# Opening of an adaptive-norm transformer block: the late conditions as one four-group product, and the queue order of the second unit's weights

## The reference

```
ada = cond @ ada_w + ada_b                       # cond 32x256, ada_w 256x1536
shift1, scale1, gate1, shift2, scale2, gate2 = split(ada, 6)
x1  = ln(x) * (1 + scale1) + shift1              # x 32x32x256
qkv = x1 @ qkv_w + qkv_b                         # 16 heads of 128
x   = x + gate1 * (softmax(q k' / sqrt(128)) v @ out_w + out_b)
x2  = ln(x) * (1 + scale2) + shift2
x   = x + gate2 * (gelu(x2 @ ffn_w1 + ffn_b1) @ ffn_w2 + ffn_b2)
out = x0 + w3q(silu(w1q(x)) * w2q(x))            # x0 the input; ternary weights, 8-bit activations
```

## Time and profile before

| | |
|---|---|
| median of 3 runs | 326.51 us (326.22 to 327.21) |
| the profiled execution | 326.65 us, of which the span from first to last instruction is 324.5 us |
| TensorE busy | 314.2 us, 97% of the span |
| VectorE, ScalarE, GpSimd busy | 224.2, 183.6 and 125.4 us |
| granted TensorE clock | 1.000 over the span |
| data moved by DMA | 24.41 MB, mean 75 GB/s |

### The profile page before, as it was taken

One profiled execution on the slowest core, in us unless ns is written; L12 is line 12 of the kernel. 1 busy time (PEld: TensorE's weight loads), 2 busy tenths in 40 slices (PEclk: granted clock), 3 DMA queues, 4 the chain that ended last, 5 costly groups with the idle time before them and its releaser, 6 DMA issues.

```text
span 324.5 us, 9866 instructions
## 1 busy us (share of the span) xinstructions
PE 314.2 (97%) x4197; PEld 281.3 (87%) x4197; DVE 224.2 (69%) x448; ACT 183.6 (57%) x356; POOL 125.4 (39%) x111
## 2 busy tenths in 40 slices
PE   8999999999999999999999999999999999997986
PEld 8979989899998989988998998879998889996665
DVE  3837885954995984515567148789177688887996
ACT  2646384555435574457434826587354866477694
POOL 2347405000940882665320612247330264115491
PEclk9999999999999999999999999999999999999999
DMA  7991990500048442110020000200110200200011
GB/s 239 299 347 56 291 319 4 150 16 2 2 110 217 127 140 96 56 45 2 3 68 4 0 26 11 66 2 2 34 34 2 65 4 2 67 0 2 0 34 65
DMA packets 21026, 24.41 MB, mean 75 GB/s; under 512 B 1972, under 2 KB 18520, under 8 KB 20984
## 3 DMA queue, kind: packets, MB, share of 16 engines
q1 hardware_dynamic: 20608, 23.50, 24.3%
q10 hardware_dynamic: 376, 0.30, 0.3%
HBM read 22.68 MB, written 1.11 MB: 73 GB/s over the span
## 4 chain that ended last, share of the span: by engine, by line
PE 83%; ACT 6%; DVE 4%; issue 2%; DMA 2%; SPq 1%; POOL 0%; DVEq 0%; ACTq 0%
PE proj_banks L570 39%; PE out_bank L570 16%; PE wide_banks L570 5%; PE turn_bank L570 4%; PE att_banks L663 3%; PE proj_banks L633 3%; PE wide_banks L855 2%; DMA stage<-in_L_cond_qkv_w 2%; PE att_banks L570 2%; ACT at_hi L1761 1%; PE wide_banks L663 1%; ACT work L1886 1%; PE att_banks L855 1%; DVE v_sb L1253 1%; PE wide_banks L738 1%
## 5 line engine op out<-in xcount | busy, mean ns | idle before, releaser
L1752 ACT ACTIVATE q_t<-proj_banks,bias_cols 128x256 f32<-128x256 f32 x64 | 30.4, 475 | 50.7 <-PE proj_banks L570 50.2
L570 PE MATMUL proj_banks<-x_hi,w_hi 128*128 128x256 f32 x252 | 54.0, 296 | 0.3 <-ACT k_t L1752 0.2
L570 PE MATMUL proj_banks<-x_lo,w_hi 128*128 128x256 f32 x252 | 50.7, 283 | 0.0
L570 PE MATMUL proj_banks<-x_hi,w_lo 128*128 128x256 f32 x252 | 50.6, 282 | 0.0
L570 PEld LDWEIGHTS proj_banks<-x_hi,w_hi 128*128 128x128 f32 x252 | 39.4, 191 | 4.1 <-issue 2.0
L570 PEld LDWEIGHTS proj_banks<-x_hi,w_lo 128*128 128x128 f32 x252 | 39.2, 191 | 0.0
L570 PEld LDWEIGHTS proj_banks<-x_lo,w_hi 128*128 128x128 f32 x252 | 39.2, 191 | 0.0
L1253 DVE TENSOR_TENSOR v_sb<-proj_banks,bv_row 128x512 f32<-128x512 f32 x32 | 21.7, 684 | 23.9 <-PE proj_banks L570 14.5
L1752 ACT ACTIVATE k_t<-proj_banks,bias_cols 128x256 f32<-128x256 f32 x64 | 30.0, 469 | 0.0
L570 PE MATMUL out_bank<-wo_hi,at_hi 128*128 128x256 f32 x128 | 21.5, 290 | 0.6
L2096 POOL TENSOR_TENSOR w_lo<-stage,w_hi 128x1024 fp32r<-128x1024 f32 x6 | 14.3, 2396 | 19.9 <-DVE w_hi L1208 14.3
(11 more groups left out here) (327 smaller groups left out, 786.2 us busy)
## 6 DMA issues: line engine op xcount, KB each, us to landing
stage<-in_L_cond_qkv_w SPq DMA_DIRECT2D x16, 256.0 KB, 4.6
gate<-gate_rows_scratch SPq DMA_DIRECT2D x48, 64.0 KB, 2.4
stage<-in_L_cond_qkv_w SPq DMA_DIRECT2D x4, 512.0 KB, 6.0
stage<-in_L_cond_out_w SPq DMA_DIRECT2D x16, 128.0 KB, 3.6
work<-in_L_ffn_w SPq DMA_DIRECT2D x2, 1024.0 KB, 9.8
xin<-in_x SPq DMA_DIRECT2D x7, 256.0 KB, 2.9
bv_row<-in_L_cond_qkv_b SPq DMA_DIRECT2D x4, 256.0 KB, 5.5
work<-in_L_cond_ada_w SPq DMA_DIRECT2D x1, 1024.0 KB, 9.9
```

The lines of the kernel that those rows point to most:

```text
L570: mm = pe.matmul(dst, l, r, start=start and i == 0, stop=stop and i == len(seq) - 1)
L1752: act.activation(dst[:, h, :], proj_bank[h % 2][:, s * QT:(s + 1) * QT], ACT.Identity, bias=bias_cols[:, c:c + 1]).then_inc(qk_kept, 1)
```

## The change

Four edits. (1) SP: `load_wo(0)` and the 1 MB transfer of `ada_w` stand behind the q and k weights of group 1; four bias rows of 32 partitions are loaded where there were two. (2) TensorE: `ada_cols` and `gates` at the end of unit 0 are replaced by `condition_rows`, which makes all four late parts as rows, eight matmuls of the form that `gates` had, each part on its own 32 PSUM partitions and so on its own group of 32 array columns. (3) VectorE adds all biases in one operation on 128 partitions (`ada_rows`, a view of `gate1`). (4) In unit 1, between heads 0 and 1, two transposes (`rows_turn`) turn the rows into columns in `wide_bank[0]`; VectorE copies shift2 and scale2 out of it (`late_conditions`) between `softmax_norm(0)` and `x1_make(1)`, and `attend(0)` waits for that. The gate rows are stored in two transfers.

```diff
             load_x(1, x_in[1])
-            load_wo(0)
             load_bv(0)
-            sp.dma_start(ada_w_sb[:, :, 2 * D:6 * D], adaw_d[:, :, 2 * D:6 * D]).then_inc(ada2_in, 16)
-            for j, c0 in enumerate((2 * D, 5 * D)):
-                sp.dma_start(gate_bias[:, j * D:(j + 1) * D], row(ada_b[c0:c0 + D], NB)).then_inc(gate_bias_in, 16)
             sp.wait_ge(projected, 1)
             for c in range(HALVES):
                 qk_split(0, c)
                 load_qk(1, c)
+            load_wo(0)
+            sp.dma_start(ada_w_sb[:, :, 2 * D:6 * D], adaw_d[:, :, 2 * D:6 * D]).then_inc(ada2_in, 16)
+            for g in range(4):
+                sp.dma_start(ada_bias[g * NB:(g + 1) * NB, :], row(ada_b[(2 + g) * D:(3 + g) * D], NB)).then_inc(
+                    gate_bias_in, 16)
             v_split(0)
             load_v(1)
...
                 if u == 0:
-                    pe.wait_ge(gate_rows_made, 1)
+                    pe.wait_ge(rows_made, 1)
+                    pe.wait_ge(ada_made, 4)
...
-            def gates():
-                pe.wait_ge(ada_made, 4)
-                for j, c0 in enumerate((2 * D, 5 * D)):
-                    for k in range(KD):
-                        mm = pe.matmul(side[0:NB, j * D:(j + 1) * D], cond_t[:, k, :], ada_w_sb[:, k, c0:c0 + D],
+            def condition_rows():
+                pe.wait_ge(ada2_in, 16)
+                for k in range(KD):
+                    for g in range(4):
+                        c0 = (2 + g) * D
+                        mm = pe.matmul(side[g * NB:(g + 1) * NB, 0:D], cond_t[:, k, :], ada_w_sb[:, k, c0:c0 + D],
                                        start=(k == 0), stop=(k == KD - 1))
-                mm.then_inc(gate_mm, 1)
+                mm.then_inc(rows_mm, 1)
+
+            def rows_turn():
+                pe.wait_ge(rows_made, 1)
+                for k in range(KD):
+                    mm = pe.transpose(wide_bank[0][:, k * P:(k + 1) * P], ada_rows[:, k * P:(k + 1) * P], ident[:, :])
+                mm.then_inc(rows_turned, 1)
...
+                if u == 1:
+                    rows_turn()
                 if u > 0:
                     qk_unit(u, 1)
...
                 v_unit(u, 1)
-                if u == 0:
-                    ada_cols(side, 3 * D, [ada2_in, ada2_in], range(2 * KD))
...
                 if u == 0:
                     x_turn(1)
-                    gates()
+                    condition_rows()
...
+            def late_conditions():
+                src = wide_bank[0][:, 0:KD * P].rearrange("p (k g b) -> p k g b", k=KD, g=4)
+                dve.wait_ge(rows_turned, 1)
+                dve.tensor_scalar(ada_t[:, 3 * KD:4 * KD, :], src[:, :, 2, :], 1.0, None, ALU.add).then_inc(ada_made, 1)
+                dve.tensor_copy(ada_t[:, 2 * KD:3 * KD, :], src[:, :, 1, :]).then_inc(ada_made, 1)
...
-                    dve.wait_ge(gate_mm, 1)
-                    dve.wait_ge(gate_bias_in, 32)
-                    dve.tensor_tensor(gate_rows, side[0:NB, :], gate_bias, ALU.add).then_inc(gate_rows_made, 1)
+                    dve.wait_ge(rows_mm, 1)
+                    dve.wait_ge(gate_bias_in, 64)
+                    dve.tensor_tensor(ada_rows, side[:, 0:D], ada_bias, ALU.add).then_inc(rows_made, 1)
...
                 if u == 1:
+                    late_conditions()
                     x1_make(1)
```

More of the change, by code:

```diff
@@ L242, in adaln_bitffn @@
         wo_stage = stage[:, WO:].rearrange("p (h d) -> p h d", h=HG)
-        gate_rows = gate1[0:NB, :, :].rearrange("p a b -> p (a b)")
-        gate_bias = xa[0:NB, :, :].rearrange("p a b -> p (a b)")
+        ada_rows = gate1[:, 0, :]
+        ada_bias = xa[:, 0, :]
         cond_rows = scores[0:NB, :, :].rearrange("p a b -> p (a b)")
@@ L302, in adaln_bitffn @@
         ada_made = sem("ada_made")
-        gate_mm = sem("gate_mm")
-        gate_rows_made = sem("gate_rows_made")
+        rows_mm = sem("rows_mm")
+        rows_made = sem("rows_made")
+        rows_turned = sem("rows_turned")
         startup_steps = sem("startup_steps")
@@ L482, in _ @@
                 sp.dma_start(dst, row(src)).then_inc(rows_in, 16)
-            sp.wait_ge(gate_rows_made, 1)
-            sp.dma_start(gate_rows_d, gate_rows).then_inc(gates_out, 16)
+            sp.wait_ge(rows_made, 1)
+            for i, g in enumerate((0, 3)):
+                sp.dma_start(gate_rows_d[:, i * D:(i + 1) * D], ada_rows[g * NB:(g + 1) * NB, :]).then_inc(gates_out, 16)
             wo_split(0)
@@ L489, in _ @@
             sp.dma_start(tern_stage[2], tern_d[2]).then_inc(tern_in[2], 16)
-            sp.wait_ge(gates_out, 16)
+            sp.wait_ge(gates_out, 32)
+            sp.wait_ge(rows_turned, 1)
             load_gate(gate1, 0, 0, gate1_in)
-            sp.wait_ge(gate_mm, 1)
+            sp.wait_ge(rows_mm, 1)
             for i in range(2):
@@ L1538, in _ @@
                         keep_v(0, t)
-                    ada_part(1, 3, side, True)
-                    ada_part(1, 3, side, False)
                     softmax_shift(0)
-                    dve.wait_ge(gate_mm, 1)
-                    dve.wait_ge(gate_bias_in, 32)
-                    dve.tensor_tensor(gate_rows, side[0:NB, :], gate_bias, ALU.add).then_inc(gate_rows_made, 1)
+                    dve.wait_ge(rows_mm, 1)
+                    dve.wait_ge(gate_bias_in, 64)
+                    dve.tensor_tensor(ada_rows, side[:, 0:D], ada_bias, ALU.add).then_inc(rows_made, 1)
                 else:
@@ L1764, in acc_keep @@
                 act.wait_ge(out_mm, 2 * (2 * Q + 2))
-                act.wait_ge(gate_rows_made, 1)
+                act.wait_ge(rows_made, 1)
                 if Q > 0:
```

## The result

The changed kernel took 331.15 us (median of 4 runs, 330.68 to 333.58) where the kernel before took 326.62 (4 runs): a ratio of 1.0139, 95% interval 1.0102 to 1.0176. It is slower by some 4.5 us. The prediction said 325.8, with a range of 324.8 to 326.9.

The account below looks back on a forecast made before the run. TensorE was taken as the bound, through unit 1's start: 3.55 us of products become 0.95 of work and 1.5 of waiting, gaining 1.0; transposes take back 0.25, net 0.75, so 325.8 us, range 324.8 to 326.9.

Parts of the forecast that it names:

- What the product waits for: TensorE before the new product: ready at 20.14, it waits for `ada_w` until 21.7, idle for 1.5 us.
- the bound from the old queue: `ada_w` landing: old q and k transfer landed 9.2 after issue, at 22.1; about 1 us dry spell makes 23.1.
- the clock, given 0.03: TensorE's wait before the product: clock falls to 1.2 GHz, slowing unit heads from 1.45 to 2.9; 329 us; chance 0.03.
- The product's 0.95: New product on TensorE: eight matmuls on four column groups take 0.95 us, between bounds 0.92 and 1.4.
- case 4: Rival, new product: four groups overlap only in pairs, taking 2.1 us; net gain -0.4, 326.9 us; chance 0.05.
- The transposes' 0.25: TensorE's path in unit 1: the two added transposes take 0.25 us with their start.
- the old order alone would leave little: Start of unit 1: with weights where they were, removing 3.55 us from TensorE could give only 0.3 us.
- v of group 1 follows 1.9 us behind `ada_w`: SP's queue: v's 640 KB at 350 GB/s land 1.9 us after `ada_w`, at 23.6, where before 23.34.
- this v has no cover on ScalarE: ScalarE before unit 1's head 2: work ends at 25.8, TensorE wants it at 25.85; later v than 23.6 loses time.
- all behind `attend(0)` shifts equally: Kernel after `attend(0)`, forecast there at 27.45 instead of 28.20: everything behind moves by the same amount.
- Case 2: Rival, SP's queue: new order costs more than the product saves; slower, 327.7 us at a 23.6 landing; chance 0.08.
- case 5: Rival, TensorE's wait: idle 1.5 us or more, the clock falls to 1.2 GHz; 329 us; chance 0.03.

Follow-up runs that it names:

- e11: Changed kernel, with SP waiting for `ada_w` to land before issuing the bias rows, group 1's v and all behind: 333.66 us, ratio 1.0213.
- e5: Changed kernel, with group 0's `out_w` transfers spread over 128 SBUF partitions instead of 32, rows in another order (not computing the reference): 329.38 us, ratio 1.0062.
- e12: Changed kernel, with SP held until `ada_w` lands and `out_w` spread over 128 partitions (not computing the reference): 331.39 us, ratio 1.0149.
- e2: Changed kernel, with eighteen filler matmuls on TensorE between the transposes and the wait for `ada_w`: 328.62 us, ratio 1.0036.
- e1: Changed kernel, with SP's old queue order restored (`out_w`, `ada_w` and bias rows ahead of group 1's q and k weights): 328.02 us, ratio 1.0021.
- e3: Changed kernel, with the four `out_w` transfers moved behind v of group 1: 328.07 us, ratio 1.0019.
- e4: Changed kernel, with `ada_w` and its four bias rows ahead of the wait for `projected`, `out_w` kept behind group 1's q and k: 325.38 us, ratio 0.9953.
- e9: Kernel before with its old products, but SP's queue in the changed order (`ada_w` and two bias rows behind q, k and `out_w`): 335.94 us, ratio 1.0273.
- e6: Kernel before with its old products; `ada_w` and two bias rows ahead of the wait for `projected`, `out_w` behind group 1's q and k: 326.53 us, ratio 0.9981.
- e7: Against e4, `out_w` also moved behind v of group 1: 324.79 us, ratio 0.9920 to the kernel before.

## Why the prediction was wrong

**The step that failed** is the landing of `ada_w`, in "What the product waits for": 21.7 was taken, 20.9 to 23.1 were the bounds, and it was 24.83. The issue times were nearly right (11.83 where 11.41 was used). The term that was mis-sized is the time of the bytes: I let 2.62 MB flow at 350 GB/s, with a slow rate for `out_w`'s own 512 KB only, which makes 8.3 us. By the same sum, 11.83 + 1.95 = 13.78, and 24.83 - 13.78 is 11.05 us: 237 GB/s for these 2.62 MB. The engines themselves moved 3.3 MB from 12 us to the landing (258 GB/s over 12.83 us), so some 0.7 MB more, for the most part issued behind `ada_w`, had moved before it landed, which the sum left out; what that cost is not shown, since e11 ended in its tail. Two more things were in the rows and not followed to their end. The slow window of the earlier trace rows was put down to `out_w`'s own bytes; e5 and e12 show that `out_w` in 32 partitions delays `ada_w` too, and the order put `ada_w` right behind it, where before it stood one transfer further off. That is 0.9 of the 3.1 us by e5; for the rest the cause stays open. And the bound from the old queue, 22.1 plus a dry spell, had the better sense of it, but was used as the far end; the dry spell was real (0.48 of the engines' time from 10 to 14 us).

**The second miss** was the clock, given 0.03. The row that was to exclude it had an idle stretch of 1.77 us, and I forecast 1.5. With the landing off by 3.1 us the stretch was 4.57, and that row said nothing on such a stretch. The two misses were treated as independent, and the second follows from the first: a late transfer lengthens the wait and then slows what follows it. The Trainium skill's rule (TensorE: Matmul & The Clock Gate, Part 1), that an idle array goes back to half its clock, agrees with this trace, where the granted clock is 0.86 and 0.71 in the windows behind the gap. By e2 it cost 1.6 us in the product and the first head.

Together: `attend(0)` was forecast at 27.45 and stood at 32.22, 4.8 later. The landing is 3.1 of it, the product 1.93 in place of 0.95, the first head 2.32 in place of 1.45; that is 4.95. Some 0.2 comes back from heads 1 and 2, which took 2.87 where the forecast left 3.05 for them. It also sized the first head too low, 1.45 for the 1.62 of e2 at the full clock.

**What was right.** The product's 0.95 (1.00 and 1.07 where the clock held: e1, e2), which also rules out case 4 with its 2.1. The transposes' 0.25 (0.22). That the old order alone would leave little: 0.3 us was said, and `attend(0)` of e1 stood at 27.87, 0.33 before, with a time not told from the kernel before. The q and k weights near 17 (17.05). That v of group 1 follows 1.9 us behind `ada_w` (1.8), though at 26.61 and not at 23.6. That this v has no cover on ScalarE: it was hidden in the changed kernel, since TensorE was later still, and set head 2 in e3 and e4. That all behind `attend(0)` shifts equally: 4.0 of 4.0 us.

**The rivals.** Case 2, the slower one, had 0.08 with 327.7 at a landing of 23.6; it is what happened, joined by case 5. Its own sum, a gain of 22.45 less the landing, gives a loss of 2.4 at 24.83 and so 328.9; e2, with the clock kept, measured 328.62. Its chance was too small: its own text named a point of 23.4 past which it decides, and the upper bound for the landing was 23.1, so 0.3 us separated a bound I had worked out from a measurable loss.

What stays open: why `out_w` in 32 partitions delays what follows it, what the transfers behind `ada_w` cost it, and where e11's tail of 3 us comes from, with which `ada_w` took 10.6 us though less was queued.

## What to carry to other kernels

A transfer's place in the queue is not only how many bytes stand ahead of it: a wait in the issuing queue can leave the DMA engines dry (0.48 busy and 156 GB/s for 4 us here), and what is moved from ahead of that wait to behind it loses the dry time as well. Fill the time ahead of the wait with the transfer that needs nothing (here e4: one 1 MB load and its bias rows moved back ahead of a wait, 5.8 us). When a wait on TensorE is lengthened, price the clock as a function of the wait, in the same case as the late arrival and not as a separate small chance.

## What the runs showed of the hardware

- TensorE's granted clock stayed at its upper level in idle stretches of 1.77 and 2.21 us (the late one of the earlier trace rows, and e3), and was at the lower level behind stretches of 2.94, 3.67, 4.57, 5.79 and 5.89 us (e12, e5, the changed kernel, e9, e11). In e9 it was 0.50 from 26 to 32 us and 1.00 again from 33.
- Loads into 32 partitions. The windows in which `out_w` lands move 230 to 284 GB/s with the engines' share at 0.99 or more, wherever it is put: 230 from 10 to 14 us before and 242 in e1; from 18 to 22 us 284 in the changed kernel, 262 in e2, 250 in e4, 238 in e7; 239 from 22 to 26 in e3. From 10 to 14 us, with `out_w` still to come, e4, e6 and e7 moved 382 to 392. Spread over 128 partitions, with the same bytes and packets, its last transfer landed at 18.8 in place of 21.7, and the windows that had 259 and 284 had 308 and 295.
- A transfer can land well after nearly all bytes of the queue have moved: in e11 `ada_w` landed at 25.6, with the engines at 0.08 of their time and 25 GB/s from 22.5 to 25.5.
- The order of landing is not that of issue: in the changed kernel the first bias row, issued at 16.2 us, landed 7.1 later, at 23.3, and `ada_w`, issued at 15.71, at 24.8.
